# Squared-relu attention: outputs kept transposed, value products spread over other slots, one multiplication of the factor removed

## What is computed

```python
queries, keys, values = (l2norm(queries), l2norm(keys), l2norm(values))
sim = jnp.einsum('bhid,bhjd->bhij', queries, keys)
attn = jnp.square(jax.nn.relu(sim))
aggr = jnp.einsum('bhij,bhjd->bhid', attn, values)
out = tanh_norm(aggr) * jnp.tanh(jax.nn.silu(gates))
return out @ Wout        # after the heads are put side by side
```

## Time and profile before

| | us |
|---|---|
| median of 3 runs (2932.36 to 2937.61) | 2934.25 |
| the profiled execution | 2932.89 |
| its span | 2931.2 |
| PE busy in the span | 2522.4 (86%) |
| DVE, ACT, POOL busy | 1959.4, 1711.9, 1178.5 |

### The profile page before, as it was taken

One profiled execution on the slowest core, in us unless ns is written; L12 is line 12 of the kernel. 1 busy time (PEld: TensorE's weight loads), 2 busy tenths in 40 slices (PEclk: granted clock), 3 DMA queues, 4 the chain that ended last, 5 costly groups with the idle time before them and its releaser, 6 DMA issues. The chain is left out here.

```text
span 2931.2 us, 38537 instructions
## 1 busy us (share of the span) xinstructions
PE 2522.4 (86%) x11350; PEld 1507.4 (51%) x11350; DVE 1959.4 (67%) x3955; ACT 1711.9 (58%) x3566; POOL 1178.5 (40%) x960
## 2 busy tenths in 40 slices
PE   7999878488898989888878999588879988898887
PEld 5777633244454544445333444356534445677775
DVE  6888755599999999999944444366534444545534
ACT  3555422499888888899722444377734434555543
POOL 1000000599999999999800000222100001444442
PEclk9999989699999999999999999799989988898988
DMA  2000032243343434444242211000012200000000
GB/s 99 2 0 1 1 109 59 87 159 144 145 159 145 157 139 152 147 151 158 108 142 59 102 58 58 0 2 0 0 44 89 85 26 1 1 1 0 0 1 15
DMA packets 34613, 205.56 MB, mean 70 GB/s; under 512 B 4000, under 2 KB 5152, under 8 KB 13216
## 3 DMA queue, kind: packets, MB, share of 16 engines
q1 hardware_dynamic: 34464, 203.83, 19.6%
HBM read 201.19 MB, written 2.62 MB: 70 GB/s over the span
## 5 line engine op out<-in xcount | busy, mean ns | idle before, releaser
L1266 POOL TENSOR_TENSOR mam_state_c<-mam_state,weights_r 128x1024 f32<-128x1024 f32 x256 | 599.8, 2360 | 67.0 <-DVE mam_state L1214 66.3
L1214 DVE TENSOR_TENSOR_SCAN mam_state<-banks,mam_dbu 128x1024 f32<-128x1024 f32 x256 | 580.2, 2277 | 5.1 <-ACT banks L1342 4.0
L1425 PE MATMUL banks<-mam_state_c,identity 128*128 128x512 f32 x1024 | 505.4, 631 | 11.5 <-POOL mam_state_c L1266 11.2
L1342 ACT ACTIVATE banks<-mam_dt,mam_a_neg 128x255 f32<-128x255 f32 x1024 | 423.8, 461 | 47.6 <-DVE mam_state L1214 45.6
L1425 PEld LDWEIGHTS banks<-mam_state_c,identity 128*128 128x128 f32 x1024 | 196.1, 201 | 232.1 <-issue 184.0
L1192 DVE TENSOR_TENSOR mam_dbu<-banks,weights_r 128x1024 f32<-128x1024 f32 x224 | 267.4, 1206 | 9.8 <-ACT banks L1350 9.8
L424 ACT ACTIVATE at_probs<-banks,at_nmax 128x256 f32<-128x256 f32 x256 | 118.0, 473 | 139.4 <-DVE at_nmax L365 139.4
L2337 POOL TENSOR_TENSOR at_attention<-at_relu 128x512 f32<-128x512 f32 x128 | 131.1, 1042 | 164.6 <-ACT at_relu L2390 86.4
L2515 PEld LDWEIGHTS banks<-at_v,at_attention 128*128 128x128 f32 x1024 | 148.1, 216 | 43.7 <-issue 35.1
L896 DVE TENSOR_TENSOR m2a_hidden<-m2a_gelu,m2a_comb_spread 128x512 f32<-128x512 f32 x120 | 80.8, 690 | 116.3 <-ACT m2a_gelu L923 113.8
L896 DVE TENSOR_TENSOR m2b_hidden<-m2b_gelu,m2b_comb_spread 128x512 f32<-128x512 f32 x120 | 80.7, 690 | 116.5 <-ACT m2b_gelu L923 113.9
(11 more groups left out here) (508 smaller groups left out, 5253.8 us busy)
## 6 DMA issues: line engine op xcount, KB each, us to landing
weights_r<-mam_bc_rows SPq DMA_DIRECT2D x128, 1024.0 KB, 4.7
m2a_comb_spread<-m2a_comb_rows SPq DMA_DIRECT2D x15, 1024.0 KB, 6.8
m2b_comb_spread<-m2b_comb_rows SPq DMA_DIRECT2D x15, 1024.0 KB, 8.1
m1a_comb_spread<-m1a_comb_rows SPq DMA_DIRECT2D x14, 512.0 KB, 7.3
m1b_comb_spread<-m1b_comb_rows SPq DMA_DIRECT2D x14, 512.0 KB, 7.1
weights_r<-in_mb SPq DMA_DIRECT2D x1, 4332.0 KB, 12.8
weights_r<-in_m SPq DMA_DIRECT2D x1, 4200.0 KB, 13.5
weights_r<-in_a SPq DMA_DIRECT2D x1, 2632.0 KB, 12.8
```

Of the source, the lines that this page charges most:

```text
L1214: dve.tensor_tensor_scan(flat2(h[:, i % 4, :, :, :]), decay(i), flat2(dbu[:, i % 4, :, :, :]), 0.0, ALU.mult, ALU.add).then_inc(h_ready, 1)
L1266: pool.tensor_tensor(hc[:, j % 4, :, :, :], h[:, j % 4, :, :, :], c_rows(j), ALU.mult).then_inc(hc_ready, 1)
L1342: i = act.activation(decay(j)[:, o + 1:o + S], dt[:, q, c, 1:S], ACT.Exp, scale=aneg[:, l, k:k + 1])
L1425: k = pe.matmul(y_bank(q)[:, :], K.ident[:, :], flat(hc[:, j % 4, n, :, :]), start=(j == 0 and n == 0), stop=(j == NP - 1 and n == 1))
```

## The change

- The product with the values is turned round: the values of one head (64 columns) are the stationary operand, and 256 columns of the attention tile are streamed. Two heads are done in one slot, every second slot, and write partitions 0 to 63 and 64 to 127 of one bank: four products for two heads in place of eight. The output has its dimensions on the partitions, as Wout needs them.
- The transposes L2499 and their copies L2414 go, and so do the sums of output squares L2294 and POOL's multiplications L2345.
- New on the PE: a product with a 0/1 matrix that sums the squares of all four groups per head (eight products of 256 columns with a stationary operand of 32 columns, slot 4), and `spread_factor`, two products of 256 columns per group that copy the factor of each head to the partitions of its dimensions (slots 8, 9 and twice in 11). DVE multiplies the gated output by it out of the bank (four of 512 columns, slots 9 to 12).
- Factor, its inverse, root, tanh and the inverse of the queries' squares now are tiles of 256 columns. The multiplication L2305 is gone; the guard is taken before the inversion; the inversion moves to slot 6, tanh to slot 6 and the last multiplication to slot 7.
- Value products are in slots 5, 6, 8 and 10, all in bank 7; the sum of squares is taken one slot later. The queries' and keys' sums move to slot 7 in bank 6 (four products of 8 columns stay, and two of 256 columns come). Scales come one slot later.
- Gate products have transposed outputs too (two of 256 columns each in place of one of 512), in banks 6 and 7 in turn. Wout's product is in bank 5, all in slot 13.
- POOL makes the 0/1 matrices once, in some 25 small instructions, ahead of the loop.

```diff
...
+        FACTOR_BANK = (4, 6, 6, 7)
...
+        VALUES = {5: 0, 6: 1, 8: 2, 10: 3}
         qk_bank = (7, 6)
-        v_bank = (7, 6, 7, 6)
-        t_bank = (6, 7, 7, 7)
...
-                    if 5 <= i < 9:
-                        n = i - 5
+                    if i - 1 in VALUES:
+                        n = VALUES[i - 1]
+                        j, c = n // 2, n % 2
+                        dve.wait_ge(v_sq, s * 4 + n + 1)
+                        dve.tensor_reduce(ss[:, 1, j, c * 8:(c + 1) * 8], heads(vsq[:, n % 2, :], 8), AX_X,
+                                          ALU.add).then_inc(v_summed, 1)
+                    if i in VALUES:
+                        n = VALUES[i]
                         j, c = n // 2, n % 2
                         dve.wait_ge(v_ps, s * 4 + n + 1)
-                        dve.tensor_copy(v[:, q, j, c * 512:(c + 1) * 512], K.ps[v_bank[n]][:, :]).then_inc(v_sb, 1)
-                        dve.wait_ge(v_sq, s * 4 + n + 1)
-                        dve.tensor_reduce(ss[:, 2, j, c * 8:(c + 1) * 8], heads(vsq[:, n % 2, :], 8), AX_X,
-                                          ALU.add).then_inc(v_summed, 1)
...
+                        dve.tensor_copy(v[:, q, j, c * 512:(c + 1) * 512], K.ps[7][:, :]).then_inc(v_sb, 1)
+                    if i == 8:
                         dve.wait_ge(nrm_ps, s + 1)
-                        link(dve.tensor_copy(ss[:, 0:2, :, :],
-                                             K.ps[7][:, 0:64].rearrange("p (a t h) -> p a t h", a=2, t=TS)))
+                        dve.tensor_scalar(rqg[:, q, :], K.ps[6][:, S:2 * S], TINY, None, ALU.max)
+                        dve.tensor_copy(ss[:, 0, :, :], K.ps[6][:, 0:32].rearrange("p (t h) -> p t h",
+                                                                                   t=TS)).then_inc(nrm_read, 1)
...
                         dve.wait_ge(nv_ready, s + 1)
-                        dve.tensor_tensor(nkv[:, :, :], ssc[:, 1, :, :], nv[:, :, :], ALU.mult).then_inc(nkv_ready, 1)
-                        dve.reciprocal(rq[:, q, :, :], ssc[:, 0, :, :])
-                    if i == 12:
+                        dve.tensor_tensor(nkv[:, :, :], ssc[:, 0, :, :], nv[:, :, :], ALU.mult).then_inc(nkv_ready, 1)
+                        dve.reciprocal(rq[:, q, :], rqg[:, q, :])
...
                         link = chain(dve, dve_s)
                         dve.wait_ge(oroot, s + 1)
-                        dve.tensor_tensor(n2[:, :, :], onn[:, :, :], rq[:, q, :, :], ALU.mult).then_inc(n_ready, 1)
-                        dve.wait_ge(n_ready, s + 1)
-                        link(dve.tensor_scalar(nmaxed[:, :, :], n2[:, :, :], 1e-12, None, ALU.max))
-                        link(dve.reciprocal(ninv[:, :, :], nmaxed[:, :, :]))
-                        link(dve.tensor_tensor(ninv[:, :, :], ninv[:, :, :], rq[:, q, :, :], ALU.mult))
+                        dve.tensor_tensor(n2[:, :], onn[:, :], rq[:, q, :], ALU.mult).then_inc(n_ready, 1)
+                        link(dve.scalar_tensor_tensor(nmaxed[:, :], rqg[:, q, :], 1e-12, onn[:, :], ALU.mult, ALU.max))
+                    if last and i == 6:
+                        s, q = last
+                        dve.reciprocal(ninv[:, :], nmaxed[:, :]).then_inc(inverse_n, 1)
+                    if last and i == 7:
+                        s, q = last
                         dve.wait_ge(th_ready, s + 1)
-                        dve.tensor_tensor(fac[:, :, :], th[:, :, :], ninv[:, :, :], ALU.mult).then_inc(fac_ready, 1)
-                    if last and i == 15:
+                        dve.wait_ge(inverse_n, s + 1)
+                        dve.tensor_tensor(fac[:, :], th[:, :], ninv[:, :], ALU.mult).then_inc(fac_ready, 1)
+                    if last and 9 <= i < 13:
+                        s, q = last
+                        g = i - 9
+                        dve.wait_ge(fac_ps, s * G + g + 1)
+                        if g == 0 and not (isinstance(s, int) and s == 0):
+                            dve.wait_ge(y_ps, s)
+                        dve.tensor_tensor(outt[:, 2 * g:2 * g + 2, :].rearrange("p c t -> p (c t)"), og[:, q, g, :],
+                                          K.ps[FACTOR_BANK[g]][:, :], ALU.mult).then_inc(outt_ready, 1)
...
-                    if last and 5 <= i < 9:
-                        s, q = last
-                        g = i - 5
-                        pool.wait_ge(fac_ready, s + 1)
-                        pool.wait_ge(og_ready, s * G + g + 3)
-                        cols = og[:, q, g, :, :].rearrange("p t (h d) -> p t h d", h=4)
-                        pool.tensor_tensor(cols, cols, fac[:, :, 4 * g:4 * g + 4].unsqueeze(3).broadcast_to([P, TS, 4, DV]),
-                                           ALU.mult).then_inc(scaled, 1)
...
-                        act.wait_ge(ot_ps, s * 4 + n + 1)
-                        act.activation(outt[:, 2 * n:2 * n + 2, :].rearrange("p c t -> p (c t)"), K.ps[t_bank[n]][:, :],
-                                       ACT.Copy).then_inc(ot_ready, 1)
...
+                            for j in range(TS):
+                                o = j * H + 8 * c
+                                pe.matmul(K.ps[6][:, o:o + 8], sq[:, c, S + j * P:S + (j + 1) * P],
+                                          eighth[:, :], start=True, stop=True)
+                        for c in range(2):
+                            k = pe.matmul(K.ps[6][:, S:2 * S], to_rows[:, c, :], sq[:, c, 0:S],
+                                          start=(c == 0), stop=(c == 1))
...
+                        if n < 2:
                             pe.wait_ge(v_sb, s * 4 + 4)
+                            pe.wait_ge(nrm_read, s + 1)
+                            if not (isinstance(s, int) and s < 2):
+                                pe.wait_ge(outt_ready, s * G - 5 + n)
                         else:
...
-                                  start=True, stop=True).then_inc(g_ps, 1)
+                            pe.wait_ge(silu_ready, s * 4 + n - 1)
+                        for b in range(2):
+                            k = pe.matmul(K.ps[6 + n % 2][:, b * S:(b + 1) * S], f("wg")[:, (2 * n + b) * P:(2 * n + b + 1) * P],
+                                          xnt[:, :], start=True, stop=True)
+                        k.then_inc(g_ps, 1)
...
+                def spread_factor(s, g):
+                    for b in range(2):
+                        k = pe.matmul(K.ps[FACTOR_BANK[g]][:, b * S:(b + 1) * S], from_rows[:, 2 * g + b, :], fac[:, :],
+                                      start=True, stop=True)
+                    k.then_inc(fac_ps, 1)
...
+                        pe.wait_ge(o_sq, s * G + G)
+                        pe.wait_ge(og_ready, s * G + G + 2)
+                        for a in range(2):
+                            for r in range(4):
+                                k = pe.matmul(K.ps[5][32 * r:32 * r + 32, 0:S], head_ones[:, a, :],
+                                              osq[:, 2 * a + r // 2, (r % 2) * S:(r % 2 + 1) * S],
+                                              start=(a == 0), stop=(a == 1))
+                        k.then_inc(on_ps, 1)
+                    if last and i == 8:
+                        s, q = last
+                        pe.wait_ge(fac_ready, s + 1)
+                        if now:
+                            pe.wait_ge(og_ready, now[0] * G + 3)
+                        spread_factor(s, 0)
...
-                        for c in range(2):
-                            for t in range(TS):
-                                k = pe.transpose(K.ps[t_bank[n]][:, c * S + t * P:c * S + (t + 1) * P],
-                                                 og[:, q, n, t, c * P:(c + 1) * P], K.ident[:, :])
-                        k.then_inc(ot_ps, 1)
...
-                    if at_:
...
+                            if g == 2 and later:
+                                pe.wait_ge(outt_ready, s * G - 3)
+                            if g == 3 and later:
+                                pe.wait_ge(done, s)
+                        for j in range(TS):
+                            for e in range(2):
+                                k = pe.matmul(K.ps[4 + g % 2][64 * e:64 * e + 64, b * S:(b + 1) * S],
+                                              v[:, q, j, (h - 1 + e) * DV:(h + e) * DV], at[:, (h - 1 + e) % 4, j, :],
+                                              start=(j == 0), stop=(j == TS - 1))
+                        k.then_inc(o_ps, 2)
...
-                            for j in range(TS):
-                                k = pe.matmul(K.ps[4 + g % 2][:, t * 256 + r * DV:t * 256 + (r + 1) * DV],
-                                              at[:, h % 4, j, t * P:(t + 1) * P], v[:, q, j, h * DV:(h + 1) * DV],
-                                              start=(j == 0), stop=(j == TS - 1))
-                        k.then_inc(o_ps, 1)
...
```

(67 more changed lines are left out.)

149 lines of the change are left out of this document (75 added, 74 removed).

## The result

The changed kernel takes 2895.61 us (median of 4 runs, 2893.26 to 2902.06) against 2935.93 for the kernel before beside it: a ratio of 0.9859, 95% interval 0.9839 to 0.9878, 40 us less. The forecast was 2883, with 2860 to 2918 as its range. The profiled execution took 2893.78 us.

The account below looks back on a forecast made before the run. PE was taken as nearest to a bound, at 88% busy. Savings of 43 (six steady sequences), 7 (first), 1.5 (preparation) and 0 (last), 51.5 us, took 2932.9 to 2881.4; with 1.4 for the median 2883, range 2860 to 2918.

Parts of the forecast that it names:

- The pair at 1.08 us: PE's four products with the values for two heads: 1.08 us at 0.27 each, saving 7.4 us a sequence.
- the reciprocal at 1.8: Two DVE reciprocals grow from 32 to 256 columns: 1.8 us each, 1.45 more than before.
- about 4 us a sequence: PE's 16 transposes that go, priced at full clock; set even with eight spread products at 3.9 us.
- PE so loses 6.3 us: PE's work per sequence falls by 6.3 us: 7.4 saved on pairs less 1.1 for sums of output squares.
- three operations go to 0.42: Three DVE operations, now of 256 columns, take 0.42 us each.
- Groups at full clock: A sequence's stretches between score products: 5.7, 11.3, and 20.7 for groups 2 and 3; 37.7 against 46.6 us.
- I add 1.8: Allowance for PE's clock falling in a steady sequence: 1.8 us on top of 37.7, giving 39.5.
- about 2 us: PE's remaining wait in group 1, for the value copy behind the factor: about 2 us.
- The one with a new chain: DVE's group 1 and the factor replace PE as bound: 42.8 to 44 us a sequence, 2911 us; chance 0.22.
- The slower one: Clock low for over half of each sequence, from a mean of about 0.7 down: 2955 us; chance 0.07.
- The clock holds: PE stays at 2.4 GHz: 37.7 us or less a sequence, 75 us saved, 2860 us; chance 0.15.
- The second rival: Narrow products don't overlap: pairs at 1.95 us, sums of squares at 3.9; about even, 2925 to 2935 us; chance 0.05.

Follow-up runs that it names:

- e5: Changed kernel with the four products with the values in the order head, then key half; 2897.74 us, ratio 0.9873.
- e2: Changed kernel with six unread filler products on PE while it waits for the first value copy; 2874.12 us, ratio 0.9777.
- e9: Changed kernel with 128 columns as stationary operand in all four products with the values, one head of two left out; 2921.08 us, ratio 0.9936.
- e6: Changed kernel with all gate products in one bank again, each waiting for silu of the one before; 2930.75 us, ratio 0.9982.
- e3: Changed kernel with the reciprocal of slot 6 done twice, the first into a spare tile; 2906.10 us, ratio 0.9887.
- e1: Changed kernel with DVE's copy of the first values ahead of the factor operations in slot 5; 2872.43 us, ratio 0.9777.
- e4: Changed kernel with DVE reading the norms ahead of the third value copy in slot 8; 2887.88 us, ratio 0.9840.
- e7: Changed kernel with the edits of e1 and e4 together; 2867.25 us, ratio 0.9766.
- e10: e7 with the inversion behind the relu of slot 7 and PE's third value product ahead of the first spread; 2859.29 us, ratio 0.9731.

## Why the prediction was right or wrong

**The time** was within the range, 13 us from the forecast, and by cause the forecast was half right.

**The sum by stretch.** Preparation 1.5 forecast, 4.0 measured; first sequence 7 and 9.9; six steady sequences 43 and 26.2; last 0 and 1.5. The misses partly cancel, which is luck: the six steady sequences alone are 17 us short.

**Prices.** The pair at 1.08 us, the sums of squares at 1.07, the reciprocal at 1.8 (1.75): right. The slope from rows of 4 and 32 columns held at 256; the estimate of 2.2 us by the Trainium skill ("VectorE: DVE Perf Modes", the first hardware budget) was too high, and the measurement decides. The halves work side by side, as I had taken it (see e5). Of the drain at a change of tiling mode, which the Trainium skill states ("TensorEngine Tiling (Array Packing)", Key Properties), the trace shows a small cost: full products of 256 columns start 0.216 us apart, also where one line follows another in the same form, and 0.309 us where a pair follows them. That is 0.09 us a change, part of the measured price of a pair; the sequence at 2646.66 has 20 such changes and the one of the earlier trace rows has 8, so by an estimate 1.1 us more. Too dear were the transposes, "about 4 us a sequence", which came from a mix of both clocks. At full clock four of them take 0.50 us, as these rows of the kernel before show, so 16 take 2.0, while the spreads, which I set even with them, took 4.0:

```profile
2695.09 0.66 PE L2499 MATMUL banks<-identity,weights_r 128*128 128x128 f32 x4 [0.64 <-DVE at_v L2258]
2695.59 1.96 PE L2459 MATMUL banks<-at_eighth_rows,at_qk_squares 128*128 128x8 f32 x16
```

"PE so loses 6.3 us" was too high by that alone; its busy time fell by 4.7, from 41.2 to 36.5. Wrong was "three operations go to 0.42": two of them ran beside POOL's square and took 0.85 and 0.54 us more.

**Groups at full clock.** I had 5.7, 11.3, 9.9 and 10.8. The changed kernel showed 5.8, 15.4, 10.3 and 10.5 and, with the clock held and nothing moved, e2 showed 5.8, 12.1, 10.5 and 10.5, a sum of 38.9 against my 37.7. Group 1 was 0.8 short, near the 0.85 that the guard took more; group 2 was 0.6 short; groups 0 and 3 came out within 0.3.

**The step that failed** is the term of the sum for the clock: "I add 1.8". I took it from the difference between sequences with a clock of 0.92 and of 0.85, but all of them had part of the fall, so that difference isn't its price; no row showed a sequence at 1.00. e2 gave the price: 3.7 us a sequence. So a steady sequence missed by 2.9 us (42.4 against 39.5): 1.7 of it is the clock, whose fall cost 3.5 of the 42.4 (38.9 without it) and not 1.8, and 1.2 the groups. In the old kernel the fall came behind the end of group 1; in the new one PE's wait stands ahead of 4 us of products that end group 1, and those took 7. I had put PE's wait at "about 2 us"; it was 3.17, and 0.85 of it is the guard beside POOL's square, which held the copy up.

**What the gain is made of.** I credited groups 2 and 3 to less work on PE. Part of it is the clock: in the sequence of the earlier trace rows the granted clock was 0.73 and 0.89 in them, and now it is 1.00. An estimate: a stretch of length T at a mean clock c loses up to T times (1 - c), which gives 5.1 us for the old groups 2 and 3, and 3.4 for the new group 1 at 0.78 (e2 measured 3.7 in the mean). By the same estimate a steady sequence lost 6.0 us before (mean clock 0.87) and 3.9 after (0.91), so about half of the 4.3 us that it gained would be clock, and half work and waits. No run holds the clock in the old kernel, so this split is not shown. e9 takes 22 us from the gain and e6 32; that is 54 for 40, so these are not parts of a sum. Both say what the new order can't do without; in e6 a fall of the clock comes on top of the wait. What the second bank would bring to the old form of the products was not tried.

**The rivals.** The one with a new chain, at 42.8 to 44 a sequence, is nearest to the measured 42.4, yet e3 shows that its reason, DVE's chain with a dearer reciprocal, isn't what held the time. The slower one named the right mechanism, the clock, with far too high a price: the mean stayed at 0.88 to 0.92, where it needed 0.7. "The clock holds" is what e1 does: 38.5, near its 37.7. The second rival, that the narrow products don't overlap, is out: their records start two at a time, and the price was 1.08.

## What to carry to other kernels

When a change makes an engine's work shorter, look at the order of its neighbour around the first wait that is left: one copy moved ahead of two operations was worth 26 us here, more than half of what the whole rewriting brought. An idle stretch of PE can cost twice, once for itself and once for the products behind it, which here ran at half pace; a filler in the wait tells in one run whether the clock or the wait is the price. When an order puts two products of one consumer next to each other, give them two banks: going back to one here took 32 of the 40 us. And an edit of the order that changes nothing doesn't prove that two units never worked side by side: look at when the records start.

## What the runs showed of the hardware

- An fp32 product with a stationary operand of 64 columns takes 0.27 us for a stream of 256 columns, with 128 columns 0.45 to 0.49. With 64 columns the records for the two halves start two at a time, 7 ns apart, and also in the order head, then key half (13 ns apart, e5); with 128 columns they start one every 0.216 us (e9).
- A change between a full product and a pair costs 0.09 us: the next record starts after 0.309 us, not 0.216. A change of line in the same form costs nothing.
- A DVE operation with two fp32 operands of 256 columns in SBUF took 0.41 to 0.43 us with no square of 128x512 on POOL, and 0.96 us where 0.68 of it lay beside one, 1.26 where 0.98 did. In both cases it ended 0.28 us behind the square, in the steady sequences of the changed kernel and of e1, e2, e4 and e7. Where an edit moved it away from the square (the guard in e1, the factor multiplication in e10) it took 0.41 and 0.42. A product with an operand in a bank (L2324, 128x512) took 0.68 wholly beside a square and 0.69 without one. No run took the square itself away. The Trainium skill ("GPSIMD Engine Reference", Specifications) states contention with DVE instructions that have two SBUF inputs; the traces agree with it.
- PE idle for 3.17 us was followed by a granted clock of 0.50 for some 6 us. With the idle stretch filled (e2) the clock stayed at 1.00. Idle for 1.44 us it stayed at 1.00 in all steady sequences of e1 and e7, but fell to 0.50 in two of six in e10 and in the first sequence of e1, so the length of the idle stretch alone doesn't decide.
